# LoRA B read over all partitions, its scratch rows in the order in which they are made, and seven moves of order in a two-layer adapter FFN kernel

## The chip, the cores and the metric

The kernel runs on one core of a Trainium2 chip. Time is device microseconds of one execution, from the first to the last instruction with what lies around them. The median of three runs is 800.48 us (798.65 to 801.49).

## The reference

The input x is 32 samples x 64 channels x 1024, that is 2048 rows of 1024 floats. All of it is float32.

```python
# layer 0
att = softmax(gelu(gelu(cond @ W0 + b0) @ W1 + b1) @ W2 + b2)          # 32 x 8
y = einsum('boi,bih->boh', einsum('bk,koi->boi', att, weight), x) + (att @ bias_k)[:, :, None]
A_eff, B_eff = einsum('bn,nri->bri', gate, lora_A), einsum('bn,nor->bor', gate, lora_B)  # 8 groups, 16 adapters, rank 32
u = y @ kernel + bias + B_eff (A_eff y) + lora_B_shared (lora_A_shared y)
x1 = x + u
# layer 1
c = grouped_conv1d(x1, 9 taps, 4 groups) + (cond @ c_weight.T)[:, :, None] + fside[None, :, None]
h1, h2 = split(c @ w12.T + b12, 2)
out = x1 + (silu(h1) * h2) @ w3.T + b3
```

## The kernel before, in words

Every product is done on pairs: an operand is split into a high part (a copy rounded to the fast float32 form, suffix `_hi`, made by ACT) and the rest (`_lo`, made by DVE as value minus high part), and three matmuls hi x hi, hi x lo, lo x hi are summed in PSUM. The five engines run programs written out by hand, one function each (`@block.sync` is SP, which issues most transfers), joined by semaphores. Nothing is scheduled by a tool: the text order of each block is the order of its engine.

**Base stage** (0 to some 90 us). SP issues, in order: two tiles of x, the eight 128-row slices of the dense kernel (`load_wk(0)` to `load_wk(7)`, 512 KB each, four buffers `raw`), LoRA A (`la_raw`, four DMAs of 512 KB), LoRA B in two halves (`load_lora_b(1)` and `load_lora_b(0)`, L399 to L404, four DMAs of 256 KB each, 32 partitions a DMA) and the shared LoRA B (`RAW_LBS`, L407). ACT makes `wk_hi` (L808) and DVE `wk_lo` (L1062) of each slice; PE runs `first_u(a, k)`, the products of row tiles 0 and 1 with slice k, as slices arrive. The LoRA B halves are transposed by DVE into `lb_t` (L1153), multiplied with the gate by `lb_result_mm(n)` on PE, and split by ACT and DVE (L820, L1158) into `lb_c`, which holds the effective B of all 8 groups: rows (k, o, group, r) over 64 partitions and two halves. Group 0 is copied from there on chip into `lb_1`, `lb_2` (`first_group_lb`, 16 small DMAs, half of them issued by ACT). All of it is stored to `lora_b_scratch` with one row block per group (L434 to L438, eight DMAs of 256 KB), from which each later group is loaded (`load_lb`, L452).

**Row tiles.** For each of 16 tiles of 128 rows: `y_tile(t)` mixes channels (PE), DVE adds the bias (`add_bias`), ACT makes `y_hi` (`split_y`, L815), DVE `y_lo` (`y_rest`). Per group of two tiles `z_group(g)` computes A y on PE and `take_z` (L1129) puts it into `z_1` and `z_2` on DVE: one cast, two subtractions and two copies. `u_tile(t)` is 24 pairs of 128x512 matmuls, `u_lora` adds the adapter's part once `lb_loaded` and `z_taken` allow it. Results go through `take_x1`, are stored to `x_scratch`, and are read back shifted for the convolution.

**Convolution and gate stage** (278 to 647 us) with 16 units `gate_unit(u)` of 7 products (a Strassen form; 12 matmuls each, L1827). Between products ACT copies partial sums out of PSUM (`part_copy`, L919), and PE may start its 3rd, 5th and 6th product only after these copies (`part_copied`). ACT also makes the next unit's weight parts (`a_hi` L887, `s_hi` L893) and the silu (L925). The vector `b12` for the silu is loaded by ACT's queue in 8 DMAs of 4-byte pieces (L862), issued after tile 3's split. The **output stage** (L1887) follows to the end.

The lines that matter most here, from SP's block and from PE's:

```python
lb_v = lora_b.rearrange("(a n) (z b e) r -> z a b n (e r)", n=4, z=2, b=32)
sp.dma_start(lb_raw[z][32 * a:32 * a + 32, :].rearrange("b (n e) -> b n e", n=4), lb_v[z, a])
...
for k in range(4, 8):
    dst, dst1 = first_u(0, k), first_u(1, k)
pe.wait_ge(lora_taken, 4 + 3)
z_group(0, 0, True)
y_tile(2, 2, 16)
y_tile(3, 3, 16)
pe.wait_ge(lb_loaded[0], LB_FIRST[0])
```

Of the kernel before, what the change touches and what calls it, by code (L numbers as in the profile page):

```python
# [50 lines left out]
def layered_kernel(nc, x, cond, fside, c0_w0, c0_b0, c0_w1, c0_b1, c0_w2, c0_b2, c0_weight, c0_bias_k,  # L51
# [17 lines left out]
    with ctx:  # L69
# [294 lines left out]
        def _(sp):  # L364
# [45 lines left out]
            load_lora_b(0)  # L410
            load_wk(5)
# [6 lines left out]
            for hl in range(2):  # L418
                sp.dma_start(lb_dram[NG, hl], lbs_c[hl][:, :]).then_inc(lbs_stored, 16)
# [14 lines left out]
            sp.wait_ge(lora_taken, N_LORA)  # L434
            for pair in range(2):
                for hl in range(2):
                    for odd in range(2):
                        sp.dma_start(lb_w[hl, odd, pair], lb_c[hl][pair][64 * odd:64 * odd + 64, :]).then_inc(lb_stored[pair], 16)  # L438

# [11 lines left out]

            def load_lb(s, src, top):  # L452
# [6 lines left out]
            def group_lb(g):  # L459
                return lb_dram[ds(g, 1)].rearrange("a h r n -> (a h r) n")  # L460
# [5 lines left out]
            for pair in range(2):  # L466
                sp.wait_ge(lb_stored[pair], 64)
            sp.wait_ge(lb_loaded[0], LB_FIRST[0])
            load_lb(1, group_lb(NG), 2 * RANK)
            load_lb(1, group_lb(1), 0)  # L470

            def rows_of_x1(i, first=False):
                for k in range(4):
                    if first and k >= 2:

                        sp.wait_ge(y_mm, 2 * k + 2)
                        sp.wait_ge(xb_made, k + 1)
                        load_x(k + 4, k)
                    store_x1(i * 4 + k, k % 2, i * 4 + k + 3)
                    if not first:  # L480

                        load_x(i * 4 + k + 4, k)
# [293 lines left out]
        def _(act):  # L776
# [87 lines left out]
            for k in range(4, 6):  # L864
                split_y(k, (k // 2) % 2, k % 2)
            with act.Fori(1, 3) as i:
                for k in range(2, 6):
                    split_y(i * 4 + k, (k // 2) % 2, k % 2)
            for k in range(2, 4):
                split_y(TILES - 4 + k, 1, k % 2)  # L870

# [162 lines left out]
        def _(dve):  # L1034
# [94 lines left out]
            def take_z(g, s, first=False):  # L1129
# [7 lines left out]
                for top in (0, 2 * RANK):  # L1137
                    a, b = slice(top, top + RANK), slice(top + RANK, top + 2 * RANK)
                    dve.tensor_tensor(z_2[s][a, :], z[a, :], z_1[s][a, :], ALU.subtract)
                    last = dve.tensor_copy(z_2[s][b, :], z_1[s][a, :])  # L1140
                last.then_inc(z_taken, 1)
# [18 lines left out]
            dve.wait_ge(yb_made, 1)  # L1160
            add_bias(0, True)
            y_rest(0, 0, 0)
            add_bias(1)
            dve.wait_ge(bias_mm, 2)
            dve.tensor_tensor(cb_c[:, :], bank(2)[0:NB, NC:2 * NC], fside_s[:, :], ALU.add).then_inc(bias_made, 1)  # L1165
            y_rest(1, 0, 1)
            wk_lo_part(1)
            la_lo_part(0)
            wk_lo_part(2)
            la_lo_part(1)  # L1170
            wk_lo_part(3)
# [412 lines left out]
        def _(pe):  # L1584
# [84 lines left out]
            def z_group(g, s, first=False):  # L1669
# [284 lines left out]
```

## Time and profile before

| | |
|---|---|
| median of 3 runs | 800.48 us |
| the profiled execution, its own time | 804.9 us |
| its span | 803.1 us |
| mean granted TensorE clock | 0.989 |
| PE busy | 779.6 us (97%) |
| DVE busy | 526.9 us (66%) |
| ACT busy | 208.9 us (26%) |
| DMA moved | 131.45 MB, mean 164 GB/s |

The table is the page's own. A busy PE is a matmul in flight, also at half clock; the remaining 3% and the stretches at half clock are where PE waited or had waited. The chain of work that ended last (81% PE, 9% DMA, 6% DVE) tells where another engine set the pace.

### The profile page before, as it was taken

What the parts mean: (1) busy time and instruction counts of PE and PEld (TensorE: products, weight loads), DVE (VectorE), ACT (ScalarE), POOL (GpSimd) and SP (SyncE); (2) the same over time, 40 slices, a digit from 0 to 9 for tenths busy, and PEclk for the clock granted to TensorE, in tenths of its full rate; (3) what the DMA queues carried; (4) which work ended last, traced back from release to release, by engine and by line L of the source; (5) the groups of instructions that cost most, each with busy time, mean ns of one, the idle gap of its engine ahead of it and who ended that gap; (6) DMA issues with size and microseconds to landing.
All of it is one profiled execution on the core that took longest, in us unless ns stands there. A gap on an engine that the chain in (4) does not pass through costs nothing.

```text
span 803.1 us, 10383 instructions
## 1 busy us (share of the span) xinstructions
PE 779.6 (97%) x3881; PEld 656.0 (82%) x3881; DVE 526.9 (66%) x636; ACT 208.9 (26%) x254; POOL 83.9 (10%) x56
## 2 busy tenths in 40 slices
PE   7988799999999999989999999999999999999998
PEld 5757688888888899868888888888888888888886
DVE  4656695436344379987777769877754796655552
ACT  5431010100000030433333337333333742111110
POOL 3141452231322100000000000000000000000000
PEclk9999999999999999989999999999999999999999
DMA  8967763464575799345444214278773664444441
GB/s 231 213 202 225 194 183 94 124 151 110 139 157 134 175 244 246 108 111 143 139 137 131 79 69 178 78 219 242 223 242 111 226 244 158 158 166 174 157 169 66
DMA packets 87275, 131.45 MB, mean 164 GB/s; under 512 B 11080, under 2 KB 64824, under 8 KB 84552
## 3 DMA queue, kind: packets, MB, share of 16 engines
q1 hardware_dynamic: 84064, 129.93, 56.1%
q10 hardware_dynamic: 3064, 0.90, 0.6%
q8 instruction: 20, 0.33, 0.2%
q0 software_dynamic: 112, 0.17, 0.1%
q14 instruction: 15, 0.12, 0.0%
HBM read 78.20 MB, written 51.72 MB: 162 GB/s over the span
## 4 chain that ended last, share of the span: by engine, by line
PE 81%; DMA 9%; DVE 6%; SPq 3%; issue 1%; ACT 1%; POOL 0%; DVEq 0%
PE ps L1827 37%; PE ps L1589 25%; PE ps L1887 19%; DMA raw<-in_L_ffn_lora_B_shared 2%; DMA raw<-in_L_ffn_kernel 2%; DVE cr L1293 2%; DMA lora_b_scratch<-lb_c_lo 1%; DMA a_scratch<-w_a_f 1%; DVE cf L1299 1%; DVE cf L1285 1%; SPq L358 1%; DMA lb<-lora_b_scratch 1%; SPq L438 1%; DMA c_scratch<-c_st 1%; DVE c_st L1299 1%
## 5 line engine op out<-in xcount | busy, mean ns | idle before, releaser
L1827 PE MATMUL ps<-cr,w_s_hi 128*128 128x512 f32 x512 | 159.8, 394 | 4.1 <-ACT s L919 4.1
L1827 PE MATMUL ps<-cr,w_a_hi 128*128 128x512 f32 x384 | 118.4, 389 | 0.0
L1827 PEld LDWEIGHTS ps<-cr,w_s_hi 128*128 128x128 f32 x512 | 97.3, 190 | 25.2 <-issue 4.9
L1827 PE MATMUL ps<-cr,w_s_lo 128*128 128x512 f32 x256 | 100.6, 393 | 0.0
L1827 PEld LDWEIGHTS ps<-cr,w_a_hi 128*128 128x128 f32 x384 | 72.0, 188 | 14.9
L1589 PE MATMUL ps<-wk_hi,y_hi 128*128 128x512 f32 x256 | 81.1, 398 | 2.0 <-DVE cb_c L1165 1.2
L1589 PE MATMUL ps<-wk_lo,y_hi 128*128 128x512 f32 x256 | 79.2, 391 | 0.0
L1589 PE MATMUL ps<-wk_hi,y_lo 128*128 128x512 f32 x256 | 78.8, 389 | 0.0
L743 POOL TENSOR_TENSOR x_t<-x_in,f_bias 128x1024 f32<-128x1024 f32 x16 | 63.5, 3973 | 137.5 <-DMA x_scratch<-x_t 137.5
L1146 DVE TENSOR_TENSOR x_t<-ps,x_t 128x1024 f32<-128x1024 f32 x16 | 19.5, 1223 | 86.7 <-PE ps L1589 86.7
L1827 PE MATMUL ps<-cr,w_a_lo 128*128 128x512 f32 x192 | 74.7, 389 | 0.0
L1518 DVE TENSOR_TENSOR res<-ps,res 128x512 f32<-128x512 f32 x56 | 38.5, 689 | 54.3 <-PE ps L1887 54.3
L815 ACT ACTIVATE y_hi<-y_f 128x512 fp32r<-128x512 f32 x32 | 19.5, 632 | 178.4 <-DVE y_f L1114 178.3
L1378 DVE TENSOR_TENSOR s<-ps,s 128x512 f32<-128x512 f32 x48 | 33.1, 689 | 41.6 <-PE ps L1827 41.3
L1589 PEld LDWEIGHTS ps<-wk_hi,y_hi 128*128 128x128 f32 x256 | 46.8, 189 | 13.0 <-issue 2.3
L1589 PEld LDWEIGHTS ps<-taps,x 128*128 128x128 f32 x512 | 57.3, 192 | 0.1
L1589 PE MATMUL ps<-taps,x 128*128 128x128 f32 x512 | 57.3, 275 | 0.0
L1827 PEld LDWEIGHTS ps<-cr,w_s_lo 128*128 128x128 f32 x256 | 48.6, 190 | 10.3
L1589 PEld LDWEIGHTS ps<-wk_lo,y_hi 128*128 128x128 f32 x256 | 48.3, 189 | 10.3
L1589 PEld LDWEIGHTS ps<-wk_hi,y_lo 128*128 128x128 f32 x256 | 48.1, 188 | 10.3
L919 ACT ACTIVATE s<-ps 128x512 f32<-128x512 f32 x48 | 28.6, 595 | 90.5 <-PE ps L1827 90.4
L925 ACT ACTIVATE s<-s,b_s 128x512 f32<-128x512 f32 x32 | 23.0, 719 | 79.7 <-DVE s L1378 79.7
(174 smaller groups left out, 1242.5 us busy)
## 6 DMA issues: line engine op xcount, KB each, us to landing
x_scratch<-x_t SPq DMA_DIRECT2D x128, 64.5 KB, 2.1
x<-x_scratch SPq DMA_DIRECT2D x32, 258.0 KB, 6.6
x_in<-in_x SPq DMA_DIRECT2D x16, 512.0 KB, 5.8
r_scratch<-r_t SPq DMA_DIRECT2D x16, 512.0 KB, 3.1
h_scratch<-s SPq DMA_DIRECT2D x32, 256.0 KB, 2.3
h_f<-h_scratch SPq DMA_DIRECT2D x8, 1024.0 KB, 5.9
res<-r_scratch SPq DMA_DIRECT2D x16, 512.0 KB, 5.0
raw<-in_L_ffn_w SPq DMA_DIRECT2D x56, 128.0 KB, 4.4
```

The lines of the kernel that those rows point to most:

```text
L743: pool.tensor_tensor(blocks(x1_t[s]), x_in[slot][:, :].rearrange("p (b h q) -> p h q b", h=2, q=4), fb_v, ALU.add).then_inc(xb_made, 1)
L815: act.activation(y_hi[s][:, a, 4 * h:4 * h + 4, :].rearrange("p k r -> p (k r)"), y_f[h][:, :], ACT.Copy).then_inc(y_hi_made, 1)
L919: act.activation((s1[u % 2], s2[u % 2], s3)[n][:, :], bank((x, x, y)[n]), ACT.Copy).then_inc(part_copied, 1)
L925: act.activation(dst[:, :], dst[:, :], ACT.Silu, bias=b12_s[:, 0, j:j + 1]).then_inc(silu_made, 1)
L1146: dve.tensor_tensor(blocks(x1_t[s]), bank(2 + 2 * s, 2).rearrange("p (b h q) -> p h q b", h=2, q=4), blocks(x1_t[s]), ALU.add).then_inc(x1 ...
L1293: dve.tensor_tensor(cr[lo][:, :, :].rearrange("p b e -> p (b e)"), cf[f][:, :, :].rearrange("p b e -> p (b e)"), cr[hi][:, :, :].rearrange ...
L1299: return dve.tensor_tensor(dst.rearrange("p (q g o) -> p q g o", q=4, g=GRP), src, c_bias[:, b * NC:(b + 1) * NC].rearrange("p (g o) -> p ...
L1378: dve.tensor_tensor(dst[:, :], bank((w, x, y)[n]), dst[:, :], ALU.add).then_inc(part_added, 1)
L1518: dve.tensor_tensor(cols, bank(OUT_BANK[b] + s), cols, ALU.add).then_inc(out_made, 1)
L1589: return pe.matmul(o, l, r, start=start, stop=stop)
L1827: last = pe.matmul(o, l, r, start=first and q == 0 and n == 0, stop=q == 3 and n == 2, skip_group_check=True)
L1887: last = pe.matmul(o, l, r, start=first and k == 0 and n == 0, stop=k == QH - 1 and n == 2, skip_group_check=True)
```

## The change

Nine edits: (1) each LoRA B half is read in four DMAs that go over all 128 partitions, one per adapter column `n`, where each went to 32 partitions; (2) the shared LoRA B is loaded first, then both halves, then kernel slice 4; (3) the scratch is written with the rows as they lie on chip (`store_lb`, four DMAs of 512 KB, two issued by ACT), and a group's rows are gathered when read; the shared part has a scratch of its own; (4) group 1's rows are loaded ahead of x tiles 4 and 5; (5) `b12` is loaded by ACT after the last tile of the base part; (6) PE runs `y_tile(2)` ahead of `z_group(0)`, and DVE `add_bias(2)` ahead of `take_z(0)`; (7) the two copies of `take_z` go to ACT (`copy_z`); (8) `conv_bias` ahead of `y_tile(1)`, `first_u(., 4)` between the two pairs of `lb_result_mm`, `la_lo_part(1)` ahead of `wk_lo_part(2)`; (9) in gate unit 0, ACT does the first two `part_copy` ahead of the next unit's weight parts and both silus last.

```diff
+    lb_dram = nc.dram_tensor("lora_b_scratch", [2 * NG * RANK, NL], F32).ap()
+    lbs_dram = nc.dram_tensor("lora_bs_scratch", [2, RANK, NL], F32).ap()
...
-        lb_w = lb_dram[0:NG].rearrange("g h (k o r) n -> h o k g r n", k=2, o=2)
+        lb_w = lb_dram[:, :].rearrange("(h k o g r) n -> h k (o g r) n", h=2, k=2, o=2, g=NG)
+        lb_g = lb_dram[:, :].rearrange("(x g r) n -> g x r n", g=NG, r=R8)
...
+        def store_lb(eng, pair):
+            eng.wait_ge(lora_taken, N_LORA)
+            for hl in range(2):
+                eng.dma_start(lb_w[hl, pair], lb_c[hl][pair][:, :]).then_inc(lb_stored[pair], 16)
...
-            lb_v = lora_b.rearrange("(a n) (z b e) r -> z a b n (e r)", n=4, z=2, b=32)
+            lb_v = lora_b.rearrange("(a n) (z b e) r -> z n a b (e r)", n=4, z=2, b=32)
             def load_lora_b(z):
-                for a in range(4):
-                    sp.dma_start(lb_raw[z][32 * a:32 * a + 32, :].rearrange("b (n e) -> b n e", n=4),
-                                 lb_v[z, a]).then_inc(lb_in[z], 16)
+                for n in range(4):
+                    cols = slice(n * 2 * PH * RANK, (n + 1) * 2 * PH * RANK)
+                    sp.dma_start(lb_raw[z][:, cols], lb_v[z, n]).then_inc(lb_in[z], 16)
+            load_raw(RAW_LBS, lora_b_s.rearrange("(b o) r -> b (o r)", b=32), rows=32)
             load_lora_b(1)
-            load_raw(RAW_LBS, lora_b_s.rearrange("(b o) r -> b (o r)", b=32), rows=32)
             store_bias(0, yb_c, yb_stored)
+            load_lora_b(0)
             load_wk(4)
-            load_lora_b(0)
...
             first_group_lb(sp, 0)
+            store_lb(sp, 0)
...
+            def load_lb(s, g):
+                src = lb_g[ds(g, 1)]
+                for n in range(2):
+                    sp.dma_start(lb_1[s][n * RANK:(n + 1) * RANK, :].bitcast(F32),
+                                 src[:, 0:4].rearrange("a x r n -> (a x) r n")).then_inc(lb_loaded[s], 16)
+                sp.dma_start(lb_2[s][0:2 * RANK, :].bitcast(F32), src.rearrange("a x r n -> (a x) r n")).then_inc(lb_loaded[s], 16)
...
+            def copy_z(g, s):
+                act.wait_ge(z_hi_made, g + 1)
+                for top in (0, 2 * RANK):
+                    last = act.activation(z_2[s][top + RANK:top + 2 * RANK, :], z_1[s][top:top + RANK, :], ACT.Copy)
+                last.then_inc(z_taken, 1)
...
-            for u in range(HALF_UNITS - 1):
+            part_copy(0, 0)
+            part_copy(0, 1)
+            a_hi(1, 0)
+            a_hi(1, 1)
+            s_hi(1, 0)
+            s_hi(1, 1)
+            part_copy(0, 2)
+            silu(0, 0)
+            silu(0, 1)
+            for u in range(1, HALF_UNITS - 1):
                 gate_unit(u)
...
-            z_group(0, 0, True)
             y_tile(2, 2, 16)
+            z_group(0, 0, True)
             y_tile(3, 3, 16)
```

SP's order before, from kernel slice 1 to slice 7 (`raw` are the slices and the shared LoRA B, `lb_raw` the two halves; the sizes are those of the written side):

```order
L368 DMA raw_84<-in_L_ffn_kernel 128x1024
L368 DMA raw_85<-in_L_ffn_kernel 128x1024
L368 DMA raw_86<-in_L_ffn_kernel 128x1024
L403 DMA lb_raw_247<-in_L_ffn_lora_B 32x4x512 x4
L368 DMA raw_83<-in_L_ffn_lora_B_shared 32x1024
L396 DMA bias_scratch<-yb_c 32x64
L368 DMA raw_84<-in_L_ffn_kernel 128x1024
L403 DMA lb_raw_246<-in_L_ffn_lora_B 32x4x512 x4
L368 DMA raw_85<-in_L_ffn_kernel 128x1024
```

and the same place in the changed program:

```order
L376 DMA raw_86<-in_L_ffn_kernel 128x1024
L376 DMA raw_83<-in_L_ffn_lora_B_shared 32x1024
L412 DMA lb_raw_247<-in_L_ffn_lora_B 128x1x512 x4
L404 DMA bias_scratch<-yb_c 32x64
L412 DMA lb_raw_246<-in_L_ffn_lora_B 128x1x512 x4
L376 DMA raw_84<-in_L_ffn_kernel 128x1024
L376 DMA raw_85<-in_L_ffn_kernel 128x1024
L404 DMA bias_scratch<-cb_c 32x64
```

Both halves now stand ahead of slice 4 (`raw_84`) and of the slices 5 to 7 behind it, and each of their DMAs is 128 partitions by one run of 512 floats.

ACT's order in gate unit 0 before (`w_a_hi`, `w_s_hi` are weight parts of unit 1; `s_..<-ps` are the copies out of PSUM; `b_s` marks a silu):

```order
L919 ACTIVATE s_0_193<-ps 128x512
L887 ACTIVATE w_a_hi_188<-w_a_f_178 128x1024
L887 ACTIVATE w_a_hi_188<-w_a_f_178 128x512
L919 ACTIVATE s_0_195<-ps 128x512
L925 ACT_TABLE_LOAD
L925 ACTIVATE s_0_193<-s_0_193,b_s 128x512
L893 ACTIVATE w_s_hi_186<-w_s_f_182 128x1024 x2
L919 ACTIVATE s_197<-ps 128x512
L925 ACTIVATE s_0_195<-s_0_195,b_s 128x512
```

and in the changed program:

```order
L943 ACTIVATE s_0_193<-ps 128x512
L943 ACTIVATE s_0_195<-ps 128x512
L911 ACTIVATE w_a_hi_188<-w_a_f_178 128x1024
L911 ACTIVATE w_a_hi_188<-w_a_f_178 128x512
L917 ACTIVATE w_s_hi_186<-w_s_f_182 128x1024 x2
L943 ACTIVATE s_197<-ps 128x512
L949 ACT_TABLE_LOAD
L949 ACTIVATE s_0_193<-s_0_193,b_s 128x512
L949 ACTIVATE s_0_195<-s_0_195,b_s 128x512
```

The second copy moved ahead of three weight parts; the third copy (`s_197`) still stands behind all of them.

## Rows read from the trace of the kernel before

**Rows 1.** Chain of waits in order of time: start us, us, what.

```profile
68.35 11.22 DMA lora_b_scratch<-lb_c_lo
...
88.54 200.03 PE ps L1589 x1064
...
292.07 10.54 DMA a_scratch<-w_a_f
...
350.31 296.65 PE ps L1827 x1296
646.96 152.90 PE ps L1887 x672
```

**Rows 2.** Timeline of PE, base stage: start us, us, instruction, idle before it.

```profile
21.14 0.72 PE L1589 MATMUL ps<-wk_hi,y_hi 128*128 128x512 f32 x2 [1.19 <-DVE cb_c L1165]
...
40.31 1.94 PE L1589 MATMUL ps<-lb_t,gate_e 128*64 128x512 f32 x8
44.48 2.96 PE L1589 MATMUL ps<-lb_t,gate_e 128*64 128x512 f32 x8 [2.23 <-DVE lb_t L1153]
...
59.52 0.28 PE L1589 MATMUL ps<-y_hi,la_g 128*128 128x256 f32 x1
...
61.44 1.95 PE L1589 MATMUL ps<-mix,x_in 128*128 128x128 f32 x16
65.46 3.51 PE L1589 MATMUL ps<-mix,x_in 128*128 128x128 f32 x16 [2.08 <-DVE y_f L1114]
...
73.37 0.63 PE L1589 MATMUL ps<-wk_hi,y_hi 128*128 128x512 f32 x2
...
88.54 2.82 PE L1589 MATMUL ps<-mix,x_in 128*128 128x128 f32 x16 [4.10 <-DMA lb<-lora_b_scratch]
...
92.86 2.03 PE L1589 MATMUL ps<-mix,x_in 128*128 128x128 f32 x16
```

**Rows 3.** DMA issues of single stretches: issuer, count, KB each, us to landing.

```profile
raw<-in_L_ffn_kernel SPq DMA_DIRECT2D x3, 512.0 KB, 14.6
...
lb_raw<-in_L_ffn_lora_B SPq DMA_DIRECT2D x4, 256.0 KB, 12.4
```

**Rows 4.** Windows: busy us of five engines, clock, DMA share of 16 engines, GB/s.

```profile
12.50:15.00 2.50, 2.50 (x12) 1.07 (x8) 1.84 (x4) 1.87 (x4) 0.85 (x1) 1.00 1.06 246
...
20.00:22.50 2.50, 1.36 (x6) 1.15 (x7) 2.38 (x5) 1.81 (x4) 0.00 (x0) 1.00 1.00 377
...
35.00:37.50 2.50, 2.50 (x21) 2.38 (x20) 1.08 (x3) 2.33 (x3) 1.51 (x1) 1.00 1.05 213
...
75.00:80.00 5.00, 5.00 (x24) 4.14 (x23) 0.71 (x3) 0.00 (x0) 0.00 (x0) 1.00 0.55 201
```

**Rows 5.** Timeline of SP's queue: issues of slices, LoRA B and its scratch.

```profile
7.99 1.57 SPq L368 DMA_DIRECT2D raw<-in_L_ffn_kernel  x3
...
24.68 1.85 SPq L403 DMA_DIRECT2D lb_raw<-in_L_ffn_lora_B  x4
...
67.71 1.24 SPq L438 DMA_DIRECT2D lora_b_scratch<-lb_c_lo  x2
```

**Rows 6.** Timelines of ACT and DVE: the last slice's high and low part.

```profile
46.64 1.06 ACT L808 ACTIVATE wk_hi<-raw 128x1024 fp32r<-128x1024 f32 x1 [0.69 <-DMA raw<-in_L_ffn_kernel]
...
52.59 2.60 DVE L1062 TENSOR_TENSOR wk_lo<-raw,wk_hi 128x1024 fp32r<-128x1024 f32 x2
```

**Rows 7.** Timelines of PE, ACT and DVE in gate unit 0, and windows.

```profile
350.31 1.19 PE L1827 MATMUL ps<-cr,w_s_hi 128*128 128x512 f32 x2 [3.39 <-ACT s L919]
...
355.56 0.77 PE L1827 MATMUL ps<-cr,w_s_hi 128*128 128x512 f32 x2
...
354.00 0.57 ACT L919 ACTIVATE s<-ps 128x512 f32<-128x512 f32 x1
...
351.77 0.69 DVE L1259 TENSOR_TENSOR w_s_f<-w_a_f,w_s_f 128x512 f32<-128x512 f32 x1
...
354.00:355.00 1.00, 1.00 (x4) 0.81 (x3) 1.00 (x2) 0.57 (x2) 0.00 (x0) 0.50 1.14 233
```

More of the change, by code:

```diff
@@ L430, in _ @@
             sp.dma_start(y_bias[:, QUART:], bias_dram[0, QUART:].partition_broadcast(P)).then_inc(bias_rest_loaded, 16)
+            wait_slot(sp, raw_of(KT - 2))
+            load_x(3, 3)
             first_group_lb(sp, 0)
+            store_lb(sp, 0)
             wait_slot(sp, raw_of(7))
             sp.dma_start(b3_s[:, :], b3.partition_broadcast(P)).then_inc(b3_in, 16)
[L434 to L438, printed above, removed]
             x8_rows = x8_dram.rearrange("k c (t n) e -> n t c k e", n=2 * GRP)
@@ L450, in store_x1, with load_lbs @@
                 sp.dma_start(r_dram[ds(t * P, P), :], r_t[s][:, :]).then_inc(r_stored[s], 16)
-            def load_lb(s, src, top):
+            def load_lb(s, g):
[4 more added lines that the diff above has]
+                sp.dma_start(lb_2[s][0:2 * RANK, :].bitcast(F32), src.rearrange("a x r n -> (a x) r n")).then_inc(lb_loaded[s], 16)
+            def load_lbs(s):
+                src, top = lbs_dram.rearrange("h r n -> (h r) n"), 2 * RANK
                 for n in range(2):
@@ L457, in load_lb @@
                 sp.dma_start(lb_2[s][top:top + 2 * RANK, :].bitcast(F32), src).then_inc(lb_loaded[s], 16)
-            def group_lb(g):
-                return lb_dram[ds(g, 1)].rearrange("a h r n -> (a h r) n")
+            for pair in range(2):
+                sp.wait_ge(lb_stored[pair], 32)
+            sp.wait_ge(lb_loaded[0], LB_FIRST[0])
+            load_lbs(1)
+            load_lb(1, 1)
             sp.wait_ge(y_mm, 4)
@@ L465, in _ @@
                 load_x(t, t - 4)
[L466 to L470, printed above, removed]
             def rows_of_x1(i, first=False):
@@ L484, in rows_of_x1 @@
                         sp.wait_ge(u_mm, i * 4 + 6)
-                        load_lb(0, group_lb(i * 2 + 2), 0)
+                        load_lb(0, i * 2 + 2)
                 sp.wait_ge(u_mm, i * 4 + 8)
-                load_lb(1, group_lb(i * 2 + 3), 0)
+                load_lb(1, i * 2 + 3)
             rows_of_x1(0, True)
@@ L856, in _ @@
             first_group_lb(act, 1)
+            store_lb(act, 1)
             split_y(2, 1, 0)
+            copy_z(0, 0)
             split_y(3, 1, 1)
+            copy_z(1, 1)
+            for k in range(4, 6):
+                split_y(k, 0, k % 2)
+            copy_z(2, 0)
+            with act.Fori(1, 3) as i:
+                for k in range(2, 6):
+                    split_y(i * 4 + k, (k // 2) % 2, k % 2)
+                    if k % 2:
+                        copy_z(i * 2 + k // 2, (k // 2) % 2)
+            for k in range(2, 4):
+                split_y(TILES - 4 + k, 1, k % 2)
+            copy_z(7, 1)
             with nc.allow_non_contiguous_dma(reason="a few columns of small arrays"):
@@ L863, in _ @@
                                       b12.rearrange("(h m j b) -> h m b j", h=2, m=4, j=NJ)[h, m]).then_inc(b12_in, 16)
[L864 to L870, printed above, removed]
             def c_hi_part(f, hi):
@@ L1137, in take_z @@
                 for top in (0, 2 * RANK):
-                    a, b = slice(top, top + RANK), slice(top + RANK, top + 2 * RANK)
-                    dve.tensor_tensor(z_2[s][a, :], z[a, :], z_1[s][a, :], ALU.subtract)
-                    last = dve.tensor_copy(z_2[s][b, :], z_1[s][a, :])
+                    a = slice(top, top + RANK)
+                    last = dve.tensor_tensor(z_2[s][a, :], z[a, :], z_1[s][a, :], ALU.subtract)
                 last.then_inc(z_taken, 1)
@@ L1168, in _ @@
             la_lo_part(0)
+            la_lo_part(1)
             wk_lo_part(2)
-            la_lo_part(1)
             wk_lo_part(3)
@@ L1189, in _ @@
             wk_lo_part(7)
+            dve.wait_ge(bias_rest_loaded, 16)
+            add_bias(2)
             take_z(0, 0, True)
-            dve.wait_ge(bias_rest_loaded, 16)
-            take_y(2, 1, 0)
+            y_rest(2, 1, 0)
             take_y(3, 1, 1)
@@ L1206, in _ @@
             for pair in range(2):
-                dve.wait_ge(lb_stored[pair], 64)
+                dve.wait_ge(lb_stored[pair], 32)
             dve.wait_ge(lb_loaded[0], LB_FIRST[0])
@@ L1673, in z_group @@
                 if not first:
-                    pe.wait_ge(z_taken, g)
+                    pe.wait_ge(z_taken, g * 2)
                 dst = bank(6)[:, 0:ROWS_G]
@@ L1699, in u_lora @@
             def u_lora(dst, t, s, a, g):
-                pe.wait_ge(z_taken, g + 1)
+                pe.wait_ge(z_taken, g * 2 + 2)
                 rows = slice(a * P, (a + 1) * P)
@@ L1740, in _ @@
             y_tile(0, 0, 16, True)
+            conv_bias()
             y_tile(1, 1, 16)
-            conv_bias()
             pe.wait_ge(bias_made, 2)
@@ L1760, in _ @@
             lb_result_mm(1)
+            dst, dst1 = first_u(0, 4), first_u(1, 4)
             pe.wait_ge(lora_taken, 4)
@@ L1763, in _ @@
             lb_result_mm(3)
-            for k in range(4, 8):
+            for k in range(5, 8):
                 dst, dst1 = first_u(0, k), first_u(1, k)
             pe.wait_ge(lora_taken, 4 + 3)
+            y_tile(2, 2, 16)
             z_group(0, 0, True)
-            y_tile(2, 2, 16)
             y_tile(3, 3, 16)
```

11 lines of the change are left out of this document (4 added, 7 removed).

## The prediction

> **What bounds the kernel now.** I read the chain of waits first. From 88.5 us on it is almost only PE: 200.0 us of row tiles, 296.7 us of gate products and 152.9 us of output [rows 1]. Between, from 292 to 350 us, a store of 10.5 us and DVE work carry it. So a microsecond saved before 88.5 us is a microsecond of the total, and a microsecond lost is too; the stages behind are shifted as they are. Next I read PE's timeline for its idle stretches. In the base stage there are four: 1.19 us for the conv bias, 2.23 us for transposed LoRA B, 2.08 us for y of tile 2, 4.10 us for group 1's LoRA B from the scratch [rows 2]. After such a wait PE also runs some 3.4 us at the lower clock: 16 mixing matmuls take 3.51 and 2.82 us there where others take 1.95 and 2.03 [rows 2]. Then I read the DMA windows, because all kernel slices and LoRA B share one queue and PE eats a slice as it comes: the last slice lands at 46.6 us (46.64, after 0.69 us of waiting for it) [rows 6]. Last I read gate unit 0, where PE idles 3.39 us [rows 7].
>
> **The change, part by part.**
>
> *The waits it aims at.* Conv bias ahead of y of tile 1: 1.2 us. The first_u step between the LoRA B products: 2.2 us, and about 1 us of low clock. y of tile 2 ahead of z: DVE now adds the bias while PE does the 1.9 us of z, 2.1 us and about 0.8 us of clock. The scratch: eight stores of 256 KB, the last two issued at 67.7 us [rows 5], landed 11.22 us after the last issue [rows 1], at 79.6 us, and the load waits for that. Four stores of 512 KB from two queues, and the load right behind them, take the 4.1 us wait away and 1.4 us of clock. If nothing else changed, that is 1.2 + 3.2 + 2.9 + 5.5 = 12.8 us; I take 12, since DVE and ACT have little room between.
>
> *How the new LoRA B read runs.* The scratch stores of the kernel before have 8 as the outermost count on the DRAM side (8 groups x 8 rows x 1024). While they alone run, from 75 to 80 us, the DMA share is 0.55 at 201 GB/s [rows 4]: about 8.8 of 16 engines, each at 201 / 8.8 = 22.8 GB/s. The LoRA A reads have 16 outermost and keep all 16 busy (share 1.06). So the number of engines follows that outermost count. The new read of LoRA B takes, for one n and z, 4 blocks (a) of 32 rows (b) of 2 KB, and a cannot be merged with b: 4 outermost. I expect 4 of 16 engines, for both halves. The Trainium skill says so in "DMA: Bandwidth & Descriptors", under why a DMA increments its semaphore by 16: the engines used are the largest number up to 16 that divides the slowest dimension of both sides, and on this queue they are the lowest-numbered ones. By that rule the stores before used 8, which the trace agrees with (share 0.55), and the read after uses 4.
>
> *How fast each of the four is.* Three rows bound it. LoRA B alone before, 35 to 37.5 us: 213 GB/s over 16, 13.3 GB/s each. LoRA A: 246 / 16 = 15.4 GB/s. Kernel slices: 377 / 16 = 23.6, and the stores 22.8 [rows 4]. LoRA A has the same kind of shape as the new read (blocks of a DRAM array spread over 128 partitions), so I take the slow side, 14.3 GB/s, the mean of 13.3 and 15.4. The two halves are 2.10 MB (2 x 4 x 256 KB [rows 3, 5]): 2.10 / (4 x 14.3) = 36.7 us; with the fast rows 2.10 / (4 x 22.8) = 23.0 us.
>
> *When they are through.* Of the three slices issued from 7.99 us [rows 5] the middle one lands 14.6 us after its issue at about 8.6 [rows 3], at 23.2 us; the next 512 KB at 377 GB/s need 1.4 us. So the four engines start on LoRA B at 24.6 us and end at T = 61.3 us. Slices 4 to 7 were issued long before, but every slice has rows on all 16 engines, and on the four they stand behind LoRA B: they land at T + 1.3, + 2.6, + 3.9, + 5.2. Twelve engines idle meanwhile. Before, slice 4 stood ahead of the second half, and that half, issued from 24.68 us, had landed by about 41 us (a median of 12.4 us from issue [rows 3, 5]).
>
> *What PE does with it.* It ends slice 3 by about 41 us and stands. Slice 4 is there at T + 1.3; ACT takes 1.06 and DVE 1.3 [rows 6], so first_u(., 4) starts at T + 3.7. Eight steps of 24 / 8 = 3 pairs follow: tile 2 has the same eight in 73.37 to 84.44 us (88.54 less 4.10), 1.37 each; two LoRA B products are 1.94 us [rows 2]. That is 12.9 us, about 1.8 us of low clock and 0.6 us for slice 6's low part come on top: y of tile 2 at T + 19. Behind it: y 1.7 (1.95 less the tail beside the next), z 1.9 (61.44 - 59.52), y 1.7, eight adapter products 1.8, 1.8 us for y_lo of tile 3, z 1.9, tile 2's eight steps 11.0 [rows 2]: tile 2 done at T + 40.8. The scratch path needs about T + 31 and is hidden. In the kernel before that point is 88.54 us plus 1.4 us of low clock behind it, 89.9. The difference is T - 49.1: with T = 61.3, **+12.2 us**. With 13.3 GB/s it is +14.9, with 15.4 it is +9.5, with 22.8 it is -1.5 and with 23.6 it is -2.3.
>
> *The groups' loads.* Each later group's lb_1 rows are read 4 blocks of 8 rows: again few engines, 24 rows of 4 KB on each of four, at most 24 x 4 KB / 14.3 GB/s = 6.9 us, issued a tile of 11 us ahead or more. Nothing; if that cover is gone, up to 2 us a group.
>
> *The z copies.* 0.3 us each off DVE, 0.5 us onto an idle ACT, behind a tile of matmuls: nothing. *b12:* 8 issues of about 1 us on ACT's queue around 255 us, ACT next needed at 283 us: nothing. Its 4-byte pieces did not slow the stores (201 GB/s beside them).
>
> *Gate unit 0.* Before, PE waits to 350.31 and runs the fifth product at half clock (0.50) until 355.56 [rows 7]. Now the second copy comes at 344 us and this product runs at once, 346.9 to 349.6. But the next needs the third copy, which stands behind the weight sums' two parts; their input is ready at 351.77 + 0.69 = 352.46 [rows 7], so it ends at about 354.4. PE then idles 4.8 us there, and runs the rest at half clock for up to 3.4 us: last product done 360.6 to 362.3, before 361.2. I take 0, bounds -0.6 and +1.1. The wait moves one product on.
>
> Sum: +12.2 us. The profiled execution has 804.9 us of its own, so 817.1; against the median 800.48, which stands 4.4 us lower, I predict **812.7 us**.
>
> **The rivals.**
>
> *Four engines at full rate* (0.28). The stores ran at 22.8 GB/s for each of 8 engines though they too walk through blocks of partitions. Then T = 47.6 and the sum is -1.5 to -2.3 us, with 2 us of doubt either way: 798.5. Within 0.3% about as often as not.
>
> *All engines share the read* (0.13). If the new read is spread over 16 engines, it has 377 GB/s and T = 24.6 + 5.6 = 30.2; then slices no longer bound PE, the 12 us of waits go, and the kernel is **faster**: 788.5. For it: the read covers 128 partitions, as the slices do, and the slices run at 377 against 213 for 32 partitions. Against it: the stores' share of 0.55 though 64 partitions were there. It decides at T = 37: below that, PE sets the pace. This is also the reading in which the change does what it says.
>
> *In between* (0.08). Two of the four collide in part, 17 to 19 GB/s: T = 54, +5 us, 805.5.
>
> *More than forecast* (0.05). Shares with the bias and shared copies behind, or slices delayed one by one so that PE drops its clock between them: +18 to +22 us, 820.
>
> **How the numbers follow.** The forecast has 0.46. Its own range is 810 to 816. About 0.3% (2.4 us) is what a measurement of this kernel can tell. Slower: 0.46 + 0.08 + 0.05 + 0.03 of the first rival = 0.62. Same: 0.12 of the first rival. Faster: 0.13 + 0.13 = 0.26. The range of 8 in 10 leaves out the second rival and the top: 795.5 to 819.
>
> **What would show it.** Right: in the changed profile the window 30 to 40 us has a DMA share near 0.25 and 55 to 65 GB/s; ACT's wk_hi of slice 4 waits for its DMA until about T + 1.3 = 62; PE idles 10 to 20 us before first_u(., 4); no PE wait for lora_b_scratch; in unit 0 the idle stretch stands before the sixth product. Wrong: a share near 1 and 350 GB/s there, slice 7 landed by 40 us, PE without a long gap before 90 us. If the share is 0.25 at about 90 GB/s, the first rival holds.

## The result, and the profile after

The changed kernel took 813.88 us (median of 6 runs, 808.78 to 818.69) beside 802.39 us of the kernel before in the same session: ratio 1.0136, 95% interval 1.0078 to 1.0195. It is slower, by 11.5 us. The forecast was 812.7 us, and slower. A second measurement (e5 below) gives 1.0120 (1.0086 to 1.0154).

The profiled execution has 818.69 us of its own and a span of 816.9 us, at the top of its runs as the one of before was near the top of its own. Clock 0.981 against 0.989; PE busy 778.9 us against 779.6. So PE's work is the same, and the time is idle PE. The chain of waits of the changed kernel, from slice 3 to tile 4:

```profile
14.09 0.64 SPq L412
...
15.39 6.37 SPq L412
...
28.14 2.45 SPq L412
...
30.64 2.32 SPq L412
...
35.50 16.99 DMA raw<-in_L_ffn_kernel
52.51 1.06 ACT wk_hi L818
...
56.05 6.27 PE ps L1622 x16
...
95.89 16.55 PE ps L1622 x88
112.43 4.54 issue
116.97 8.23 PE ps L1622 x40
...
367.15 293.37 PE ps L1861 x1284
```

In the kernel before, PE's 200 us of tiles begin in this chain at 88.54 and nothing breaks them [rows 1]. Now a slice lands at 52.5 us where the last of all was there at 46.6 [rows 6]. Its transfer takes 17 us from its issue, and the issue itself stands behind LoRA B on SP's queue. That queue (start, duration, issue, count):

```profile
13.71 0.34 SPq L376 DMA_DIRECT2D raw<-in_L_ffn_lora_B_shared  x1
14.09 10.72 SPq L412 DMA_DIRECT2D lb_raw<-in_L_ffn_lora_B  x4
24.86 2.65 SPq L404 DMA_DIRECT2D bias_scratch<-yb_c  x1
27.54 7.91 SPq L412 DMA_DIRECT2D lb_raw<-in_L_ffn_lora_B  x4
35.50 3.00 SPq L376 DMA_DIRECT2D raw<-in_L_ffn_kernel  x2
```

Before, four such issues took 1.85 us [rows 5]; now 10.72 and 7.91, and even the 8 KB of `bias_scratch` 2.65. The issues are not alike: the first of a group take some 0.6 us, one takes 6.37, and those of the second half behind the first 2.3 to 2.5. The windows of the changed kernel, columns as in [rows 4]:

```profile
25.00:30.00 5.00, 5.00 (x26) 3.92 (x25) 4.36 (x5) 1.54 (x2) 0.00 (x0) 1.00 0.27 97
30.00:35.00 5.00, 5.00 (x35) 4.49 (x33) 1.75 (x2) 1.53 (x2) 2.10 (x1) 1.00 0.26 102
...
40.00:45.00 5.00, 1.00 (x6) 0.12 (x2) 0.00 (x0) 0.00 (x0) 0.00 (x0) 0.88 1.05 242
```

A share of 0.26 is 4.2 of 16 engines, and they move 102 GB/s: 24 GB/s each. From 40 us on, with the slices issued, all 16 run, and the rate is 242 / 16 = 15 GB/s each. PE's timeline of the changed kernel, with the idle time in front:

```profile
56.05 1.19 PE L1622 MATMUL ps<-wk_hi,y_hi 128*128 128x512 f32 x2 [15.05 <-DVE wk_lo L1095]
...
66.74 0.70 PE L1622 MATMUL ps<-wk_hi,y_hi 128*128 128x512 f32 x2 [0.63 <-DVE wk_lo L1095]
...
95.89 2.02 PE L1622 MATMUL ps<-mix,x_in 128*128 128x128 f32 x16 [0.96 <-issue]
...
116.97 0.55 PE L1622 MATMUL ps<-y_hi,la_g 128*128 128x256 f32 x1 [4.54 <-issue]
...
353.82 0.70 PE L1861 MATMUL ps<-cr,w_s_hi 128*128 128x512 f32 x2 [0.44 <-ACT s L943]
...
367.15 1.19 PE L1861 MATMUL ps<-cr,w_s_hi 128*128 128x512 f32 x2 [4.89 <-ACT s L943]
```

The 15.05 us are where the forecast had them, the four waits of [rows 2] are gone or under 1 us (conv bias, `lb_t`, y of tile 2, scratch), and in unit 0 the idle stretch stands before the sixth product and not the fifth, 4.89 us against 3.39 [rows 7].

### The profile page after: what moved, and what is told of

It reads as the page before. It is cut to its first block, busy times and chain, and to the rows that moved or that the text cites. A ratio compares the mean times of both kernels' runs of the same rounds, so it can differ in the third digit from the quotient of the medians.

```text
span 816.9 us, 10383 instructions
## 1 busy us (share of the span) xinstructions
PE 778.9 (95%) x3881; PEld 655.3 (80%) x3881; DVE 518.8 (64%) x620; ACT 215.6 (26%) x270; POOL 81.0 (10%) x56
## 4 chain that ended last, share of the span: by engine, by line
PE 83%; DVE 7%; DMA 4%; SPq 3%; issue 2%; ACT 1%; POOL 0%; ACTq 0%; DVEq 0%
PE ps L1861 36%; PE ps L1622 28%; PE ps L1921 19%; DMA raw<-in_L_ffn_kernel 3%; SPq L412 2%; DVE cr L1326 2%; DMA a_scratch<-w_a_f 1%; DVE cf L1332 1%; DVE cf L1318 1%; DVE c_st L1332 1%; DVE w_a_f L1276 1%; SPq L537 0%; SPq L404 0%; DVE y_lo L1154 0%; POOL wk_lo L736 0%
## 5 line engine op out<-in xcount | busy, mean ns | idle before, releaser
L753 POOL TENSOR_TENSOR x_t<-x_in,f_bias 128x1024 f32<-128x1024 f32 x16 | 61.7, 3859 | 140.7 <-DMA x_scratch<-x_t 140.7
L1861 PEld LDWEIGHTS ps<-cr,w_s_lo 128*128 128x128 f32 x256 | 48.5, 189 | 10.3
```

The costliest lines, as they stand in the source:

```text
L753: pool.tensor_tensor(blocks(x1_t[s]), x_in[slot][:, :].rearrange("p (b h q) -> p h q b", h=2, q=4), fb_v, ALU.add).then_inc(xb_made, 1)
L1861: last = pe.matmul(o, l, r, start=first and q == 0 and n == 0, stop=q == 3 and n == 2, skip_group_check=True)
```

## The experiments

Ratios are to the kernel before in the same session, with the 95% interval.

| | kernel | median us | ratio |
|---|---|---|---|
| | changed | 813.9 | 1.0136 (1.0078 to 1.0195) |
| e1 | changed, LoRA B read as before | 795.2 | 0.9939 (0.9914 to 0.9964) |
| e2 | before, with the new read | 813.2 | 1.0151 (1.0119 to 1.0182) |
| e3 | changed, third copy early | 813.6 | 1.0147 (1.0109 to 1.0184) |
| e4 | changed, x 4 and 5 first | 810.0 | 1.0113 (1.0083 to 1.0143) |
| e5 | changed, again | 810.0 | 1.0120 (1.0086 to 1.0154) |
| e6 | changed, read in small pieces | 794.9 | 0.9926 (0.9898 to 0.9954) |
| e7 | e1 and e4 | 795.2 | 0.9920 (0.9893 to 0.9947) |
| e8 | e7 and e3 | 794.8 | 0.9914 (0.9882 to 0.9946) |
| e9 | e8, partial add early | 789.0 | 0.9833 (0.9810 to 0.9857) |
| e10 | before, again | 800.8 | 0.9988 (0.9965 to 1.0011) |
| e11 | e1, unit 0 as before | 791.7 | 0.9886 (0.9854 to 0.9918) |

### The read alone (e1, e2, e6)

```diff
 e1, from the changed kernel
-            lb_v = lora_b.rearrange("(a n) (z b e) r -> z n a b (e r)", n=4, z=2, b=32)
+            lb_v = lora_b.rearrange("(a n) (z b e) r -> z a b n (e r)", n=4, z=2, b=32)
-                for n in range(4):
-                    cols = slice(n * 2 * PH * RANK, (n + 1) * 2 * PH * RANK)
-                    sp.dma_start(lb_raw[z][:, cols], lb_v[z, n]).then_inc(lb_in[z], 16)
+                for a in range(4):
+                    sp.dma_start(lb_raw[z][32 * a:32 * a + 32, :].rearrange("b (n e) -> b n e", n=4),
+                                 lb_v[z, a]).then_inc(lb_in[z], 16)
```

> The changed kernel with one thing undone: each LoRA B half is again read in four DMAs of 32 partitions (one per a); the order of SP's queue and all else stay. Theory 1 (the four-engine read sets the base stage): the window 25 to 35 us moves over 200 GB/s at a DMA share near 1 in place of 100 GB/s at 0.26, SP issues a LoRA B DMA in about 0.45 us in place of 2.4 us, slice 4's copy on ACT comes at about 37 to 40 us in place of 52.5, and PE's 15.05 us wait before first_u(., 4) falls below 3 us. The kernel takes 795 to 801 us, 1 to 7 us below the kernel before; what keeps it from more are the waits of 0.96 and 4.54 us at tile 4 and group 2 and the unit 0 wait. Rival 2 (the order of the queue, LoRA B ahead of slice 4, is what costs, whatever the number of engines): slice 4 still comes after both halves at 45 us or later, the wait stays over 8 us, and the time is 807 us or more.

Measured 795.2 us, ratio 0.9939: theory 1. Windows, slice 4 on ACT, and SP's queue of e1:

```profile
25.00:30.00 5.00, 5.00 (x26) 3.92 (x25) 3.92 (x5) 1.55 (x2) 0.00 (x0) 1.00 1.06 220
...
35.00:40.00 5.00, 5.00 (x28) 3.35 (x27) 2.40 (x5) 3.55 (x4) 1.75 (x3) 1.00 1.03 369
```

```profile
36.22 1.06 ACT L818 ACTIVATE wk_hi<-raw 128x1024 fp32r<-128x1024 f32 x1 [3.29 <-DMA raw<-in_L_ffn_kernel]
```

```profile
13.29 1.85 SPq L411 DMA_DIRECT2D lb_raw<-in_L_ffn_lora_B  x4
```

The same bytes at the same place in the queue now have 16 engines and 220 GB/s. Each engine is slower (13.8 GB/s), together they are twice as fast, and slice 4 is there 16 us earlier. PE's 15.05 us wait is gone altogether, and SP issues the first four in 1.85 us again. From 35 us on, when the slices run, the same 16 engines move 369 GB/s, 23 each.

> The kernel before with edit 1 alone: the LoRA B halves read over 128 partitions, in the old place of the queue (half 1, shared part, slice 4, half 0, slice 5). Theory 1: four engines at 24.5 GB/s each need 10.7 us a half; half 1 from 24.6 to 35.3, slice 4 at 36.7, half 0 to 47.4, slices 5 to 7 at 48.7, 50.0 and 51.4 us, where they had landed by 46.6; SP is held 2.4 us an issue. PE's wait before first_u(., 5) is some 5 us, the waits behind stay: 806 to 811 us, slower than before by 4 to 9 us but less than the full change's 11.5. Rival 2 (the read costs only in the changed order): within 2 us of the kernel before.

(The diff of e2 is that of e1 read the other way, on the kernel before.) Measured 813.2 us, ratio 1.0151, 12 us: the sign of theory 1, but more than its 4 to 9 us. e2's queue, PE and DVE say why:

```profile
9.51 14.54 SPq L404 DMA_DIRECT2D lb_raw<-in_L_ffn_lora_B  x4
24.09 2.65 SPq L368 DMA_DIRECT2D raw<-in_L_ffn_lora_B_shared  x1
```

```profile
44.87 3.68 PE L1589 MATMUL ps<-lb_t,gate_e 128*64 128x512 f32 x8 [4.98 <-DVE lb_t L1153]
...
55.46 3.68 PE L1589 MATMUL ps<-lb_t,gate_e 128*64 128x512 f32 x8 [6.91 <-DVE lb_t L1153]
```

```profile
37.80 2.08 DVE L1173 STREAM_TRANSPOSE lbs_t<-raw 32x1024 f32<-32x1024 f32 x1 [8.97 <-DMA raw<-in_L_ffn_lora_B_shared]
...
52.58 2.73 DVE L1153 STREAM_TRANSPOSE lb_t<-lb_raw 128x256 f32<-128x256 f32 x8 [6.07 <-DMA lb_raw<-in_L_ffn_lora_B]
```

I had counted only the slices behind the second half. But SP was held 14.54 us over the first four issues, so the shared part, for which DVE waits ahead of the transposes, was not issued until 24 us: DVE stood 8.97 us for it and PE 4.98 us before its first LoRA B products. The second half came only at 52.6 us, where I had 47.4: DVE stood 6.07 us for it and PE 6.91. Of the waits behind, which were to stay, the one for the scratch is not in this profile. Edit 1 alone costs 12 us on the old order; taken out of the changed kernel it is worth more: 1.0136 to 0.9939, or 1.0120 to 0.9939 by e5, 14.5 to 16 us of 802.

```diff
 e6, from the changed kernel (DVE's wait goes from 64 to 256)
-            lb_v = lora_b.rearrange("(a n) (z b e) r -> z n a b (e r)", n=4, z=2, b=32)
+            lb_v = lora_b.rearrange("(a n) (z b e) r -> z n a b (e r)", n=4, z=2, b=32)
-                    sp.dma_start(lb_raw[z][:, cols], lb_v[z, n]).then_inc(lb_in[z], 16)
+                    for a in range(4):
+                        sp.dma_start(lb_raw[z][32 * a:32 * a + 32, cols], lb_v[z, n, a]).then_inc(lb_in[z], 16)
```

> The changed kernel with each of the LoRA B DMAs, still one per n, cut into four of 32 partitions, so that b (32) and not a (4) is the outermost count; the runs of 2 KB, the bytes and the order by n stay. Theory 1 (the outermost count picks the engines): the DMA share from 20 to 30 us is near 1 at over 200 GB/s, the wait before first_u(., 4) falls under 3 us; 32 issues of some 0.45 us are 14 us of SP, from 13 to 28 us, so slice 4 is issued about 3 us later than in e1: 795 to 801 us. Rival 2 (reading one n at a time, in pieces 2 KB long with strides, is what runs slowly): about 100 GB/s again and 807 us or more.

Measured 794.9 us, ratio 0.9926: theory 1. Window and queue of e6:

```profile
25.00:30.00 5.00, 5.00 (x25) 3.89 (x25) 4.04 (x4) 1.54 (x2) 0.00 (x0) 1.00 1.08 271
```

```profile
13.45 7.38 SPq L413 DMA_DIRECT2D lb_raw<-in_L_ffn_lora_B  x16
```

The order by n, the runs of 2 KB and their strides are those of the changed kernel. Only the outermost count went from 4 to 32, and the share went from 0.27 to 1.08, the rate from 97 to 271 GB/s, SP's time for a half's issues from 10.72 us to 7.38, though there are four times as many (0.46 us each, of 64 KB). So neither the order by n nor the runs are at fault. One thing went with the count: each DMA of e6, as of e1, covers 32 partitions and not 128. A DMA of 128 partitions with another outermost count was not tried on LoRA B; the slices cover 128 partitions and have a share of 1.00 [rows 4], and the old scratch stores, 8 outermost over 64 partitions, have 0.55, so the span alone does not explain the four engines, and the outermost count fits all of these rows.

### The waits behind it (e4, e5, e7, e10)

```diff
 e4, from the changed kernel
+            sp.wait_ge(y_mm, 4)
+            sp.wait_ge(xb_made, 2)
+            for t in (4, 5):
+                load_x(t, t - 4)
             for pair in range(2):
                 sp.wait_ge(lb_stored[pair], 32)
             sp.wait_ge(lb_loaded[0], LB_FIRST[0])
             load_lbs(1)
             load_lb(1, 1)
-            sp.wait_ge(y_mm, 4)
-            sp.wait_ge(xb_made, 2)
-            for t in (4, 5):
-                load_x(t, t - 4)
```

> The changed kernel with x tiles 4 and 5 loaded ahead of the wait for the scratch stores and of group 1's rows (edit 4 undone). Theory 1: the 0.96 us wait at tile 4's mixing goes, since its x is issued at about 80 us in place of 88.25; the stores of x1 start only 0.9 us earlier, so the 4.54 us wait before z_group(2) stays above 3 us: 1 to 2.5 us less than the changed kernel, about 812 us. Rival 2 (x tiles behind the group load are the whole cause of both waits): both go, with their half clock, 6 to 7 us less, 807 us.

> The changed kernel once more, to have its time and a second profile beside the other kernels. Theory: 812 to 815 us; PE's wait before first_u(., 4) is again 14.5 to 15.5 us (e3 and e4 had 15.1 and 14.7). The wait before z_group(2), 4.5 us in the first profile and 3.1 us in e3, is there again between 3 and 5 us if it comes from the order of SP's queue; if it was a mishap of one execution, it is gone.

e4 took 810.0 us and its profile has neither wait, which alone would speak for rival 2. But e5, the changed kernel with nothing altered, took 810.0 us too and has them no more. PE of e5, then its mixing of tile 4, and that of e4:

```profile
53.31 1.19 PE L1622 MATMUL ps<-wk_hi,y_hi 128*128 128x512 f32 x2 [12.83 <-DVE wk_lo L1095]
...
109.40 0.36 PE L1622 MATMUL ps<-y_hi,la_g 128*128 128x256 f32 x1 [0.40 <-issue]
```

```profile
92.55 1.95 PE L1622 MATMUL ps<-mix,x_in 128*128 128x128 f32 x16
```

```profile
92.54 1.95 PE L1622 MATMUL ps<-mix,x_in 128*128 128x128 f32 x16
```

Tile 4 begins at 92.55 in e5 and 92.54 in e4. Both theories of e4 fall: the two waits belonged to the first execution (its 4.54 us, and 3.14 in e3), not to edit 4, which costs nothing that can be measured.

> e1 and e4 together: LoRA B read in 32-partition DMAs, x tiles 4 and 5 loaded ahead of the group's rows. In e1 the waits at tile 4 and z_group(2) were already only 0.5 us. Theory 1: same as e1 within 1.5 us (795 us), since the queue is early there anyway. Rival 2 (the order alone is worth e4's 4 us): 791 us.

e7 took 795.2 us, as e1: theory 1. (Its diff is e1's and e4's together.)

How the 4.54 us of the first execution came about can be read there. POOL and DVE in the changed kernel:

```profile
111.71 3.81 POOL L753 TENSOR_TENSOR x_t<-x_in,f_bias 128x1024 f32<-128x1024 f32 x1 [2.79 <-DMA x_scratch<-x_t]
```

```profile
98.56 1.47 DVE L1154 TENSOR_TENSOR y_lo<-y_f,y_hi 128x512 fp32r<-128x512 f32 x2
104.49 1.23 DVE L1178 TENSOR_TENSOR x_t<-ps,x_t 128x1024 f32<-128x1024 f32 x1 [4.46 <-POOL x_t L753]
105.75 5.21 DVE L1235 TENSOR_TENSOR r_t<-x_t,b_s 128x1024 f32<-128x1024 f32 x1
...
112.30 4.57 DVE L1154 TENSOR_TENSOR y_lo<-y_f,y_hi 128x512 fp32r<-128x512 f32 x2 [0.16 <-ACT y_hi L825]
```

The x1 stores were late, POOL's additions behind them too; DVE waited 4.46 us for one, and its two `y_lo` (1.47 us at 98.56) took 4.57 us while POOL worked beside them, so PE got y_lo at 116.97. In e5 POOL's addition came at another time, and the same two took 1.29 us:

```profile
108.01 1.29 DVE L1154 TENSOR_TENSOR y_lo<-y_f,y_hi 128x512 fp32r<-128x512 f32 x2 [0.16 <-ACT y_hi L825]
```

So the wait is there when POOL's addition meets these two, in the first profile and in e3 (4.89 us for them), and gone when it does not. Why the stores were late in the one execution is not shown.

> The kernel before, to have a second profile. Its first profiled execution had 804.9 us against a median of 802. Theory: the four base stage waits (1.19, 2.23, 2.08, 4.10 us) are in this one too, each within 1 us, and the unit 0 wait is 3.4 us: 801 us. Rival: one or more of them were of that execution only, and then the 12 us counted for them were too many.

e10 took 800.8 us. Of the four waits two are smaller in this execution, one by 1.40 us and one by 0.80: 1.19, 0.83, 1.28 and 4.16 us, 7.5 in all against 9.6 [rows 2]:

```profile
43.69 1.90 PE L1589 MATMUL ps<-lb_t,gate_e 128*64 128x512 f32 x7 [0.83 <-DVE lb_t L1153]
...
61.72 2.02 PE L1589 MATMUL ps<-mix,x_in 128*128 128x128 f32 x16 [1.28 <-DVE y_f L1114]
...
84.10 3.47 PE L1589 MATMUL ps<-mix,x_in 128*128 128x128 f32 x16 [4.16 <-DMA lb<-lora_b_scratch]
```

So none is gone, one is off by more than the 1 us of the theory, and the rival holds in part. e5 and e10 are also the better pair to compare, both near their medians (809.4 and 800.5 us of their own): gate unit 0's first product starts at 337.67 against 330.36, 7.3 us of the difference of 8.9. The gate stage, 1.9 us longer by the stretch compared below, holds the rest.

### Gate unit 0 (e3, e8, e9, e11)

```diff
 e3, ACT, from the changed kernel (e8: the same on e7)
             a_hi(1, 1)
+            part_copy(0, 2)
             s_hi(1, 0)
             s_hi(1, 1)
-            part_copy(0, 2)
```

> The changed kernel with ACT's third copy in gate unit 0 moved ahead of unit 1's two weight sums (s_hi), behind a_hi. Theory 1: the third copy was held only by ACT's order; PE's 4.89 us wait before the sixth product goes, and with it some 2 us at half clock: 6 to 7 us less than the changed kernel, 807 us. As the copy still stands behind a_hi, whose last input came at 361.8 us, PE may wait up to 0.5 us. Rival 2 (a wait takes its place: the copy is then held by the store of c or by h, or unit 1's first product waits for the weight sums): at most 2 us less, 812 us or more.

> e7 with the third copy of unit 0 ahead of unit 1's weight sums, as in e3. Unit 0, from its first product to unit 1's first, took 24.3 us in the changed kernel and 21.9 in e3, but some of it came back as half clock in unit 1 (311.9 against 312.8 us from the first product to the output stage). Theory 1 (DVE sets unit 1's start): 0.9 us less than e7. Rival 2 (ACT's order sets it): 4 us or more less.

e3 took 813.6 us and e8 794.8, neither to be told from its base. The 4.89 us went, and 3.87 us appeared one product on, for another engine. PE and DVE of e3:

```profile
357.19 0.70 PE L1861 MATMUL ps<-cr,w_s_hi 128*128 128x512 f32 x2 [0.81 <-ACT s L943]
364.06 0.70 PE L1861 MATMUL ps<-cr,w_a_hi 128*128 128x512 f32 x2 [3.87 <-DVE s L1411]
```

```profile
359.81 2.36 DVE L1299 TENSOR_TENSOR w_s_lo<-w_s_f,w_s_hi 128x1024 fp32r<-128x1024 f32 x2 [0.47 <-ACT w_s_hi L917]
362.09 1.22 DVE L1309 TENSOR_TENSOR w_a_lo<-w_a_f,w_a_hi 128x1024 fp32r<-128x1024 f32 x1
363.23 0.69 DVE L1411 TENSOR_TENSOR s<-ps,s 128x512 f32<-128x512 f32 x1
```

Rival 2 was right that a wait takes its place, but named the wrong one: the row at 364.06 is unit 0's seventh product (the expectation of e8 calls it unit 1's first, which is wrong), and it waits for DVE's second partial add. That add could have run at about 357.2 us, and stood behind three low parts of unit 1's weights. So one line more was moved:

```diff
 e9, DVE, from e8
                 weight_sums(u + 1)
+                if u == 0:
+                    part_add(0, 1)
                 s_lo(u + 1, 0)
                 s_lo(u + 1, 1)
                 a_lo(u + 1, 0)
-                part_add(u, 1)
+                if u:
+                    part_add(u, 1)
```

> e8 with DVE's second partial add of unit 0 (part_add(0, 1)) moved from behind the low parts of unit 1's weights to right behind the weight sums. In e3 and e8 PE waited 3.87 and 3.90 us for this add before unit 0's seventh product, though its inputs had been there some 6 us. Theory 1 (DVE's order sets it): that wait falls to at most 0.5 us and the half clock behind it goes; unit 1 may then wait up to 1.5 us for the low parts, which come 0.6 us later: 2.5 to 4.5 us less than e8, 791 to 792 us. Rival 2 (DVE has no room there, the wait reappears whole before unit 1): no change against e8.

e9 took 789.0 us, ratio 0.9833: 13 us below the kernel before and the fastest of all; theory 1, and with 5.9 us below e8 some more than its 2.5 to 4.5. PE of e9:

```profile
337.26 0.70 PE L1864 MATMUL ps<-cr,w_s_hi 128*128 128x512 f32 x2 [0.81 <-ACT s L943]
...
340.16 0.70 PE L1864 MATMUL ps<-cr,w_a_hi 128*128 128x512 f32 x2
...
344.16 0.72 PE L1864 MATMUL ps<-cr,w_a_hi 128*128 128x512 f32 x2 [1.01 <-DVE w_a_lo L1311]
```

The seventh product (340.16) follows the sixth at once, 1.01 us is left before unit 1, and PE no longer drops its clock (1.00 from 328 to 352 us; e5 had 0.50 from 357 to 363). From the first gate product to the first output product, no other wait being in that stretch, e9 takes 307.7 us and the six profiles with edit 9's order (the changed kernel twice, e1, e4, e6, e7) 312.4 to 313.5.

```diff
 e11, ACT, from e1
-            part_copy(0, 0)
-            part_copy(0, 1)
...
-            for u in range(1, HALF_UNITS - 1):
+            for u in range(HALF_UNITS - 1):
                 gate_unit(u)
```

> e1 with edit 9 undone: ACT's order in gate unit 0 as in the kernel before. Theory 1 (the wait only moves one product on): the wait of 4.9 us before the sixth product becomes 3.4 us before the fifth; from the first product of unit 0 to the seventh 22.2 to 23.7 us as before, against 24.3 to 24.5; the time is that of e1 less 0.6 us, not to be told from it (795 us). Rival 2 (edit 9 gains, as fewer products stand behind the first copies): 1 us or more above e1.

e11 took 791.7 us (0.9886) against 795.2 (0.9939) of e1; the intervals just touch. The same stretch takes 310.3 us in e11, 310.6 in e2, 311.6 in e10 and 312.0 in the first profile, mean 311.1; with edit 9's order the mean is 312.8. So edit 9 costs about 1.7 us; the profiles of one order differ by up to 1.8 us among themselves, but no two of the two orders overlap. It has the sign of theory 1, whose 0.6 was too small, and the other sign than a gain. The rest of the 3.5 us between e11 and e1 is not explained.

## Why the prediction was right

**Where the time is set.** Right. e1 leaves all behind the base stage as it is and takes 15 us out of it.

**Four of 16 engines.** Right: share 0.26, and e6, with 32 outermost and the same runs in the same order, has a share of 1.08. The Trainium skill ("DMA: Bandwidth & Descriptors", under why a DMA increments its semaphore by 16) gives 4 for the one and 16 for the other, and the trace agrees both times.

**How fast each of the four is.** This step failed. I took 14.3 GB/s, from rows in which all 16 engines ran; the four alone ran at 24 to 25 GB/s each (97 to 103 GB/s). By the prediction's own signs it was the first rival's rate that held (a share of 0.25 at about 90 GB/s), and not the forecast's 55 to 65 GB/s. The same array with all 16 running gave 220 / 16 = 13.8 (e1), so what is read did not by itself call for the slow row. (Nor was the row from 35 to 37.5 us LoRA B alone: SP had issued slices 5 to 7 between 27.44 and 35.3 us.) But the slices with all 16 running gave 23 to 24 (369 in e1, 377 in [rows 4]), so the number of engines at work does not set the rate alone either; what holds 16 engines on LoRA B to 14 stays open. The row to take was the stores' 22.8. For the figure alone: the same page, under "Specifications", states about 27 GiB/s for an engine, which is 29 GB/s; the four reach about 0.85 of it.

**When they are through.** T was to be 61.3; by slice 4 (52.5 less 1.3) it was 51.2 in the first profile and 48.5 in e5, where ACT had it at 49.76. The sign named for it, ACT's copy of slice 4 at about 62 us, did not come. The first rival's T was 47.6, 1 to 4 us under what came. Neither had that SP's queue is held while the four engines are behind, so that slices 4 and 5 were issued only from 35.5 us. From 40 us on all 16 engines ran, at 15 GB/s each (242 / 16), and I take it that the rest of the second half went at that rate too, which is a reading of the window and not of the four engines by themselves.

**What PE does with it.** The sum said tile 4 begins at T + 40.8, which is 92.0 with T = 51.2 and 89.3 with 48.5; it began at 95.89 and 92.55, 3.3 to 3.9 us later. 1.1 of it is the step from slice 4 to the first product (3.54 us against 2.4): DVE makes LoRA A's last low part ahead of slice 4's, and waits for ACT, which makes its high part behind that of slice 4. The order is that of the kernel before, and I had left it out. Most of the rest are waits that I had at nothing: 1.44 (group 0's rows) and 0.38 us in e5; 1.06, 0.72 and 0.96 in the first profile. The wait of 0.63 to 0.66 us for slice 6's low part was in the sum with 0.6. PE's long wait was 12.83 to 15.05 us. That lies in the 10 to 20 named as a sign, but the sum itself, with PE done by 41 us and the first product at T + 3.7 = 65.0, makes it 24: the sign fitted the rival's rate and was no support for the forecast.

**The waits it aims at.** 12 us were too many. With the old read unit 0's first product starts at 322.32 us (e1) against 330.36 in e10, 8.0 us earlier. In time the other edits together gain 5 us (e1), and 9 without edit 9 (e11). The forecast summed the waits of one execution; in a second one two of the four were 2.2 us smaller together, and with the old read PE still waits 0.66, 1.57 and 0.5 us.

**The groups' loads, z copies, b12.** Nothing, as far as is shown: from the product at 116.97 us (in e5 at 109.40) to unit 0 PE has no idle stretch in either profile of the changed kernel, so no product waits for a group's rows or for z. e4 and e7 change only where group 1's rows stand in the queue. None of the three was tried alone.

**Gate unit 0.** The wait moved one product on and is 4.89 us, as forecast (4.8). I took 0 with bounds -0.6 and +1.1; it is +1.7.

**The sum.** For the two first executions it reads: +12.2 as forecast, -10.1 for T (51.2), +3.9 for tile 4's lateness, which is +6.0 at tile 4 (95.89 against 89.9); +4.5 for the wait of that execution and +2.4 for the half clock behind it, +12.9 when tile 5 is mixed (its mixing ends at 123.1 against 110.2); about 1 in the gate stage: 818.7 against 804.9, +13.8. For e5 and e10 it reads: +12.2 as forecast, -12.8 for T (48.5), +3.3 for tile 4's lateness, +4.4 because the kernel before is at tile 4 that much earlier in e10 (84.10 and its 1.4 us of low clock, 85.5, against 89.9): +7.1 at tile 4; with unit 0, +8.9. So the predicted time is good to 1.2 us by luck: a rate that was too low, worth 10 to 13 us, stood against waits that I had at nothing or counted in full. The sign was right for its own reason, the four engines. With the stores' rate and nothing else changed the sum would have been -1.5 us, and wrong.

## What to carry to other kernels

Look at the outermost count on the DRAM side of every DMA, not at how many partitions it covers: 4 put the read on 4 engines, and its price is paid by whatever stands behind it in the same queue, at the issue as well as on the engines. A rate per engine must come from a row that is like the transfer both in what is moved and in how many engines are at work: LoRA B had 24 GB/s an engine on four and 14 on 16, the slices 23 on 16. And an order of waits is cleared only when the next engine's order is read too: moving one copy on ACT gained nothing until DVE's add, one product on, was moved with it.

## What had not been expected of the hardware

DMAs confined to four engines hold the issuing queue: four issues of 256 KB took 10.72 and 7.91 us in place of 1.85, one of them 6.37 us (in e2 four took 14.54), and an 8 KB store issued among them 2.65 us. In the second half three issues in a row took 2.3 to 2.5 us, about what four engines need for 256 KB at 102 GB/s (2.6 us, an estimate), so I read them as issues at the pace of the engines. Twelve engines idled meanwhile (share 0.26).

One engine reached 24 to 25 GB/s with three others, and 13.8 to 17 with fifteen, on the same array and the same 2 KB runs; e6, which changes the block of partitions with every DMA, had 271 GB/s where e1, with all four n of one block in a DMA, had 220. Why was not tried.

DVE's two `y_lo`, 1.29 to 1.47 us when POOL was idle, took 4.57 us beside POOL's addition here. The Trainium skill ("SBUF — State Buffer", under who interferes with whom) has a port pair that the two share and lock; the trace agrees in that DVE's operations end at 116.87, after POOL's is over (115.52).
